# Sixteen-head attention: key and query roots of a head taken as one block, with a first guess from ScalarE

## The reference, cut to what matters

```python
def rmsnorm(x, g, eps=1e-05):
    var = jnp.mean(jnp.square(x), axis=-1, keepdims=True)
    return x * jax.lax.rsqrt(var + eps) * g
q = (hidden_states @ Wq).reshape(B, Sq, H, D)
k = (encoder_hidden_states @ Wk).reshape(B, Skv, H, D)
v = (encoder_hidden_states @ Wv).reshape(B, Skv, H, D)
q, k = rmsnorm(q, gq), rmsnorm(k, gk)
scores = jnp.einsum('bqhd,bkhd->bhqk', q, k) / np.sqrt(D)
out = jnp.einsum('bhqk,bkhd->bqhd', jax.nn.softmax(scores, axis=-1), v)
x = x + jnp.tanh(g) * (out.reshape(B, Sq, H * D) @ Wo)
```

## Time and profile before

| | |
|---|---|
| median of 3 runs | 4504.84 us (4497.9 to 4512.92) |
| span of the profiled execution | 4504.5 us |
| instructions | 38786 |
| TensorE busy | 3722.7 us, 83% |
| VectorE busy | 3377.8 us, 75% |
| ScalarE busy | 1500.6 us, 33% |
| mean granted TensorE clock | 0.909 |

### The profile page before, as it was taken

The page is one execution under the profiler, slowest core; times in us unless marked ns, Lnnn a source line. Parts: engine busy times, 40 slices in busy tenths (PEclk is TensorE's granted clock), DMA queues, the critical chain, the costliest instruction groups (busy, mean ns, idle before and its releaser), DMA issues.

```text
span 4504.5 us, 38786 instructions
## 1 busy us (share of the span) xinstructions
PE 3722.7 (83%) x11597; PEld 1853.8 (41%) x11650; DVE 3377.8 (75%) x5902; ACT 1500.6 (33%) x2273; POOL 375.2 (8%) x329
## 2 busy tenths in 40 slices
PE   5555555699999967999938997999999999999656
PEld 1222222244444433443423443665665664664222
DVE  6999999798898724898897554773773773774887
ACT  3433333233233222334400111552552552551322
POOL 0000000043242101333100000000000000000000
PEclk7787777799999978999969998999999999999888
DMA  2211121423323211433420001110110110110000
GB/s 93 71 47 66 47 70 38 147 102 125 145 103 119 70 56 56 152 136 139 145 112 22 1 0 59 36 42 23 38 40 23 40 38 23 39 38 32 10 10 19
DMA packets 74467, 289.30 MB, mean 64 GB/s; under 512 B 8848, under 2 KB 17168, under 8 KB 60592
## 3 DMA queue, kind: packets, MB, share of 16 engines
q1 hardware_dynamic: 59440, 220.09, 14.1%
q0 software_dynamic: 14848, 67.12, 4.4%
HBM read 261.48 MB, written 25.69 MB: 64 GB/s over the span
## 4 chain that ended last, share of the span: by engine, by line
PE 48%; DVE 34%; issue 12%; ACT 3%; DMA 2%; DVEq 0%; SPq 0%; POOL 0%; POOLq 0%; ACTq 0%
PE ps L831 34%; DVE room L1323 6%; PE ps L1117 5%; DVE room L1321 3%; PE ps L1108 2%; PE ps L939 2%; PE ps L989 2%; DVE room L1261 2%; DVE room L1265 1%; DVE stat L1225 1%; DVE room L1269 1%; DVE room L1288 1%; DMA room<-bc_scratch 1%; DVE ln L1239 1%; DVE stat L1712 1%
## 5 line engine op out<-in xcount | busy, mean ns | idle before, releaser
L831 PE MATMUL ps<-room 128*128 128x512 bf16 (+1 forms) x2809 | 930.9, 489 | 121.9 <-ACT room L779 49.0
L831 PE MATMUL ps<-lnT,room 128*128 128x512 f32 x2240 | 988.1, 597 | 19.4 <-DVE room L1458 12.0
L831 PEld LDWEIGHTS ps<-room 128*128 128x128 bf16 (+1 forms) x2848 | 390.0, 140 | 638.1 <-issue 318.7
L831 PEld LDWEIGHTS ps<-lnT,room 128*128 128x128 f32 x2240 | 426.4, 191 | 538.7 <-issue 498.9
L867 PE MATMUL ps<-room,ident 128*128 128x512 f32 x512 | 342.8, 833 | 334.5 <-DVE room L1327 334.4
L493 POOL TENSOR_TENSOR idle<-idle 128x1 f32<-128x1 f32 x160 | 284.2, 1776 | 1885.1 <-DVE xres L1247 1080.7
L939 PE MATMUL ps<-room 128*128 128x512 f32 x864 | 377.0, 593 | 8.5 <-DVE room L1410 8.5
L867 PEld LDWEIGHTS ps<-room,ident 128*128 128x128 f32 x512 | 132.5, 271 | 544.2 <-DVE room L1327 379.7
L1323 DVE TENSOR_TENSOR_SCAN room<-room 128x2048 f32<-128x2048 f32 x64 | 283.2, 4425 | 6.4
L555 ACT ACTIVATE room<-room,small 128x511 f32<-128x511 f32 x256 | 163.8, 711 | 372.8 <-DVE room L1265 359.0
L1265 DVE TENSOR_TENSOR_SCAN room<-room 128x2048 f32<-128x2048 f32 x64 | 283.4, 4428 | 5.7 <-DVE room L1261 0.5
(11 more groups left out here) (206 smaller groups left out, 4609.6 us busy)
## 6 DMA issues: line engine op xcount, KB each, us to landing
room<-bc_scratch SPq DMA_DIRECT2D x128, 256.0 KB, 4.0
room<-in_ffn SPq DMA_DIRECT2D x16, 2048.0 KB, 10.9
room<-bc_scratch POOLq DMA_DIRECT2D x128, 256.0 KB, 3.6
room<-in_head SPq DMA_DIRECT2D x64, 512.0 KB, 3.6
room<-stash POOLq DMA_DIRECT2D x24, 1024.0 KB, 9.2
room<-in_ffn SPq DMA_DIRECT2D x20, 1024.0 KB, 5.7
room<-in_ffn SPq DMA_DIRECT2D x12, 1536.0 KB, 8.0
stash<-room SPq DMA_DIRECT2D x12, 1024.0 KB, 5.9
```

The source lines that it names most:

```text
L831: last = nc.tensor.matmul(out, lhsT, rhs, start=(i == 0), stop=(i == len(parts) - 1))
```

## The change

VectorE no longer takes two separate roots in a head. The sums of the keys' squares and of the queries' squares come to lie side by side in a 128x8 block (`square_keys` and the first line of `normalize`). ScalarE takes Ln of the block and then Exp with scale -1/2 (`root_guess`), with a wait on its own semaphore between them. VectorE makes one Newton step on the block and then scales the keys. So the scaling of the keys, which came before the query sums and did not depend on them, now follows them. `round_bit` goes between `square_keys` and `normalize`. ScalarE's `root_guess` stands behind the four copies of the transposed softmax and before `take_kT`; at a batch start it stands between `take_q` and `take_kT`. TensorE's stream is the same but for the name of a semaphore.

```diff
--- before.py
+++ after.py
@@ -227,11 +227,12 @@
         a_exp, a_P_ready, a_tr, a_PT_ready, a_x = sem("a_exp"), sem("a_P_ready"), sem("a_tr"), sem("a_PT_ready"), sem("a_x")
 
         h_wloaded = [sem("h_wloaded0"), sem("h_wloaded1")]
-        h_wo_loaded, h_qss_used = sem("h_wo_loaded"), sem("h_qss_used")
+        h_wo_loaded = sem("h_wo_loaded")
         h_kvp, h_kv_raw, h_ksum, h_kn, h_ktr, h_kT_ready = (
             sem("h_kvp"), sem("h_kv_raw"), sem("h_ksum"), sem("h_kn"), sem("h_ktr"), sem("h_kT_ready"))
         h_qp, h_q_ready, h_qss, h_s, h_max, h_exp, h_P_ready = (
             sem("h_qp"), sem("h_q_ready"), sem("h_qss"), sem("h_s"), sem("h_max"), sem("h_exp"), sem("h_P_ready"))
+        h_var, h_rs0 = sem("h_var"), sem("h_rs0")
         h_tr, h_PT_ready, h_pv, h_out_ready, h_proj = (
             sem("h_tr"), sem("h_PT_ready"), sem("h_pv"), sem("h_out_ready"), sem("h_proj"))
 
@@ -717,7 +718,7 @@
 
             def attention3(stage):
                 P3, PT3 = t3(h_P, NT), t3(h_PT, NT)
-                rs, nb, total, gqk = stat[:, 100:104], stat[:, 104:108], stat[:, 108:112], stat[:, 112:113]
+                rs, nb, total, gqk = stat[:, 92:96], stat[:, 104:108], stat[:, 108:112], stat[:, 112:113]
 
                 def take_kv(b, h):
                     hh = b * H + h
@@ -731,6 +732,12 @@
                     nc.scalar.activation(h_q, ps[:, 3, :], ACT.Copy)
                     nc.scalar.activation(h_sq, ps[:, 3, :], ACT.Square).then_inc(h_q_ready, 1)
 
+                def root_guess(b, h):
+
+                    act.wait_ge(h_var, b * H + (h + 1))
+                    chain.link(nc.scalar.activation(stat[:, 56:64], stat[:, 80:88], ACT.Ln))
+                    nc.scalar.activation(stat[:, 88:96], stat[:, 56:64], ACT.Exp, scale=-0.5).then_inc(h_rs0, 1)
+
                 def take_kT(b, h):
                     act.wait_ge(h_ktr, b * H + (h + 1))
                     nc.scalar.activation(h_kT[h % 2], ps[:, 2, :], ACT.Copy, scale=gqk).then_inc(h_kT_ready, 1)
@@ -741,6 +748,7 @@
                     take_lnT(stage, b)
                     take_kv(b, 0)
                     take_q(b, 0)
+                    root_guess(b, 0)
                     take_kT(b, 0)
 
                 def body(b, last):
@@ -756,14 +764,16 @@
                             act.wait_ge(h_tr, (b * H + h) * NT + (k + 1))
                             nc.scalar.activation(PT3[:, k, :], ps[:, 4 + k, :], ACT.Copy).then_inc(h_PT_ready, 1)
                         if h + 1 < H:
+                            root_guess(b, h + 1)
                             take_kT(b, h + 1)
                         act.wait_ge(h_pv, b * H + (h + 1))
                         nc.scalar.activation(h_out3[:, h, :], ps[:, 0, :], ACT.Copy).then_inc(h_out_ready, 1)
                     if not last:
                         start(b + 1)
                 act.wait_ge(x_done, B * stage)
+                chain.start, chain.k = chain.start + chain.k, 0
                 start(0)
-                batches(act, body)
+                chain.batches_peeled(H, H - 1, body)
 
             def bitnet(stage):
                 dq1, sc2, rnd = stat[:, 116:120], stat[:, 132:134], stat[:, 134:135]
@@ -1051,7 +1061,7 @@
                         _, wkv = weights(h)
                         pe.wait_ge(h_wloaded[h % 2], b * (H // 2 * 16) + (h // 2 + 1) * 16)
                         pe.wait_ge(h_out_ready, b * H + max(h - 1, 0))
-                        pe.wait_ge(h_qss_used, b * H + h)
+                        pe.wait_ge(h_var, b * H + h)
                         for t in range(NT):
                             mm = product(ps[:, t // 2, (t % 2) * 256:(t % 2) * 256 + 256],
                                          [(ctx3[:, c, t * P:(t + 1) * P], wkv[:, c, :]) for c in range(CK)])
@@ -1622,29 +1632,30 @@
 
             def attention3(stage):
                 P3, PT3 = t3(h_P, NT), t3(h_PT, NT)
-                rs, nb, total, inv = stat[:, 100:104], stat[:, 104:108], stat[:, 108:112], stat[:, 76:80]
-                ksums, krms, ktmp = stat[:, 80:84], stat[:, 84:88], stat[:, 48:56]
-                qsums, qrms, qtmp = stat[:, 88:92], stat[:, 92:96], stat[:, 56:64]
-                mx = stat[:, 68:72]
+                nb, total, inv = stat[:, 104:108], stat[:, 108:112], stat[:, 76:80]
+                ksums, qsums, sums = stat[:, 80:84], stat[:, 84:88], stat[:, 80:88]
+                krms, rs, roots = stat[:, 88:92], stat[:, 92:96], stat[:, 88:96]
+                rtmp, mx = stat[:, 48:56], stat[:, 68:72]
                 ksq = t3(h_ksq, NT)
 
-                def norm_keys(b, h):
+                def square_keys(b, h):
 
                     dve.wait_ge(h_kv_raw, b * H + (h + 1))
                     k = t3(h_kv[h % 2], NT)[:, :, 0:HD]
                     link(v.tensor_tensor(ksq, k, k, ALU.mult))
                     link(v.tensor_reduce(ksums, ksq, AX.X, ALU.add))
                     link(v.tensor_scalar(ksums, ksums, 1.0 / HD, EPS, ALU.mult, ALU.add))
-                    rsqrt(krms, ksums, NT, ktmp)
+
+                def normalize(b, h):
+
+                    dve.wait_ge(h_qss, b * H + (h + 1))
+                    v.tensor_scalar(qsums, ps[:, 1, 0:NT], HD * EPS, None, ALU.add).then_inc(h_var, 1)
+                    dve.wait_ge(h_rs0, b * H + (h + 1))
+                    link(v.scalar_tensor_tensor(out=rtmp, in0=roots, scalar=-0.5, in1=roots, op0=ALU.mult, op1=ALU.mult))
+                    link(v.tensor_tensor(rtmp, rtmp, sums, ALU.mult))
+                    link(v.scalar_tensor_tensor(out=roots, in0=rtmp, scalar=1.5, in1=roots, op0=ALU.add, op1=ALU.mult))
+                    k = t3(h_kv[h % 2], NT)[:, :, 0:HD]
                     v.tensor_tensor(k, k, krms.unsqueeze(2).broadcast_to([P, NT, HD]), ALU.mult).then_inc(h_kn, 1)
-
-                def query_scales(b, h):
-
-                    dve.wait_ge(h_qss, b * H + (h + 1))
-                    v.tensor_scalar(qsums, ps[:, 1, 0:NT], 1.0 / HD, EPS, ALU.mult, ALU.add).then_inc(h_qss_used, 1)
-                    dve.wait_ge(h_qss_used, b * H + (h + 1))
-                    rsqrt(qrms, qsums, NT, qtmp)
-                    link(v.tensor_scalar(rs, qrms, HD**-0.5, None, ALU.mult))
 
                 bit_sum, bit_mean, bit_inv = stat[:, 120:124], stat[:, 124:128], stat[:, 148:152]
 
@@ -1679,13 +1690,14 @@
                             link(v.reciprocal(inv[:, t:t + 1], total[:, t:t + 1]))
                             v.tensor_scalar(P3[:, t, :], P3[:, t, :], inv[:, t:t + 1], None, ALU.mult).then_inc(h_P_ready, 1)
                         if h + 1 < H:
-                            norm_keys(b, h + 1)
-                            query_scales(b, h + 1)
+                            square_keys(b, h + 1)
                         round_bit(b, h)
+                        if h + 1 < H:
+                            normalize(b, h + 1)
                     if not last:
                         layernorm(stage, b + 1)
-                        norm_keys(b + 1, 0)
-                        query_scales(b + 1, 0)
+                        square_keys(b + 1, 0)
+                        normalize(b + 1, 0)
                     elif stages > 7:
                         dve.wait_ge(h_pv, B * H)
                         bit_front(0)
@@ -1696,9 +1708,9 @@
                 dve.wait_ge(x_done, B * stage)
                 bit_scales()
                 layernorm(stage, 0)
-                norm_keys(0, 0)
-                query_scales(0, 0)
-                KEYS = 3 + 11 + 11 + 1
+                square_keys(0, 0)
+                normalize(0, 0)
+                KEYS = 3 + 3
                 n = H * (2 * NT + 2) + (H - 1) * KEYS
                 chain.batches_peeled(n + LN_LINKS + KEYS, n + (FRONT if stages > 7 else 0), body)
 
```

## The result

The changed kernel takes 4727.2 us (median of 4 runs, 4725.2 to 4732.1), the kernel before 4503.6 (4 runs, 4497.9 to 4512.9): ratio 1.050, 95% interval 1.048 to 1.051. The forecast was 4727.

What follows compares the result with a forecast made beforehand. The prediction took TensorE to bound the heads. Stalls of 132 us, clock loss 72, batch ends 15 and start 3 sum to 222; with 4504.5 and 0.3 that gives 4727 us, range 4632 to 4778.

Steps and rivals of the forecast that it cites:

- TensorE bounds the heads, VectorE's relief is worth nothing: Stage 6 heads: TensorE is busy all 17.02 us, so the some 4.2 us a head that VectorE sheds gain nothing.
- Two loads a head, the second in the middle of the chain: ScalarE in each head: one table load ahead of Ln, one ahead of the new Exp, 1.29 us each.
- The first load does not wait for the sums: ScalarE in each head: the load ahead of Ln starts when the last copy of the transposed softmax ends, 2974.69.
- The stall: TensorE before the next head's key transposes: waits 2.2 us (2.1 to 2.4) for scaled keys, 60 times, 132 us.
- the whole stall reaches the end: After the key transposes the scores are late next, so all 2.2 us of TensorE's wait lengthen each head.
- The granted clock: TensorE behind its wait in the heads: half speed costs 1.7 us in two heads of three, 1.2 a head, 72 us.
- The reading that a stall near 1 us costs no clock: From the trace before: TensorE's wait of 0.95 us at 3144.56 shows no fall of the clock.
- Batch ends and start: First head's key transposes wait 3.3 us, 5.0 with clock, at three batch ends, 15 us; stage start 3 us.
- A drain around each load: Rival, chance 2%: ScalarE empties around each load for about 1.28 us, two a head, 154 us more, 4881 us.
- One table for both functions: Rival, chance 5%: no loads in the heads, the change hidden there, 8 us left at batch ends and start, 4513 us.
- The faster rival: Rival, chance 2%: at batch ends VectorE, relieved, frees the last head's softmax sooner; four waits of 2.1 us go, 4488 us.

## Why the prediction was right, step by step

**TensorE bounds the heads, VectorE's relief is worth nothing:** right. VectorE shed 219 us of work (forecast some 230; the product 64 x 22 x 0.16 gives 225), and with the same work shed and the loads gone the time is 4518.5, no less than before.

**Two loads a head, the second in the middle of the chain:** right, 128 in the trace. The evidence was stage 0, where Exp and Ln alternate with a load each. Changing only which table is loaded took 209 us away, so this is shown, not argued.

**The first load does not wait for the sums:** right, it starts 0.02 us behind the copies.

**The stall:** its idle time was forecast at 2.2 and is 2.29. What was missed is TensorE's filling after a stall, 0.2 us: the step "the whole stall reaches the end" should have read 2.5 a head. It is 151 us in place of 132; of the 19 more, 13 are the filling and the rest the longer idle time.

**The granted clock:** the mechanism and the frequency were right, the price of a fall was not. I took two heads in three at 1.7 us, which is 68 us and became 72 by rounding 1.13 to 1.2. The trace has 37 of 56 intervals with a fall, two in three, at 1.44 us: 53 us. I had priced a fall as 3.4 us full of work. In the head at 2970.79 windows of 0.5 and 1 us put the half speed from about 2970.6 to 2974.0, so its first 0.2 us passed in the stall. The transposes grow by 0.46 us there, the value products by 0.85 and the score products behind by 0.06. The four transposes need 0.65 at full speed and 1.11, not 1.30, at half, so the filling seems not to double. Why the score products lose 0.06 us in their 0.37 us at half speed, and not 0.19, is not shown. The reading that a stall near 1 us costs no clock held at 1.01 us.

**Batch ends and start:** forecast 18 us. Between the first key transposes of the stage and its last ones the changed kernel takes 218 us more. With 151 and 53 taken away, 14 are left for the batch ends and the start, and 2 more of the 220.5 between the two profiled spans lie outside. The idle times are there as forecast (3.4 us at L1078).

Counted on the profiled spans, the errors are +19, -19 and -4, with 2 outside the stage, and they cancel to less than 2; the medians of the runs differ by 223.6. By its parts the forecast was good to some 20 us, and that the total came out at 4727 is luck to that extent.

**The rivals.** A drain around each load: refuted by the 1.28 us between a head with one load and one with two, by a load that starts 0.02 us behind the copies, and by activations that start 0.01 us behind their load. The Trainium skill (ScalarE: Activation LUTs, What ACT_TABLE_LOAD costs) adds about 1.38 us to each switch. The trace does not agree: there a switch costs its load of 1.28 us and nothing more. One table for both functions exists and works once it is loaded by hand, 4518.5 us, where 4513 had been worked out; the batch ends and the start cost 14 us there and not 8. The Trainium skill describes such a set (ScalarE: Activation LUTs, Table sets: the hidden batching unit). The faster rival did not happen in this change. TensorE's waits for the softmax at the batch ends, before and after (us in all, times, longest), are nearly the same although VectorE had less to do:

```profile
PE ps L1108 <- DVE room L1680: 9.2, 15, 1.6
...
PE ps L1118 <- DVE room L1691: 9.5, 16, 1.6
```

But the place that it named held 27 us, which came back by giving TensorE work there, not by relieving VectorE.

## What to carry to other kernels

Before work moves to ScalarE, look in the trace whether the two functions alternate anywhere already, and whether a load stands before each: two activations of 0.21 us brought two loads of 1.28. What a load costs depends on who waits: the same 128 loads cost 22 us beside the chain and over 200 in it. On an engine that is 100% busy count a stall as idle time, plus filling, plus what the clock loses. When a shared bank is used to fill a hole, ask at once who has to empty it and behind what that one waits.

## What the runs showed of the hardware that was not expected

A stall costs about 0.2 us more than its idle time, since the four transposes behind it hold the chain for 0.65 us and not 0.44; heads with stalls of 0.58, 1.01 and 2.29 us all show it (17.83, 18.25 and 19.53 us against 17.02). A stall of 1.01 us in each head left the granted clock at 1.00, one of 2.29 lowered it in two heads of three (37 of 56 intervals), one of 3.57 in all 56. One fall behind a stall of 2.29 us cost 1.4 us. Loading a table that is already active takes the same 1.28 us as a switch.
